# An image block with a selective scan and attention: rotation by partition halves, unrolled attention, and SyncE's scan-stage jobs in thirds

## The chip, the cores and the metric

The kernel runs on one core of one Trainium2 chip. The metric is the device time of a run in microseconds (us), lower is better. A core has TensorE (PE in the profile; its weight loads are PEld), VectorE (DVE), ScalarE (ACT), GpSimd (POOL) and SyncE (SP), which here only issues DMAs.

## The reference

The input is four images of 32x32 tokens with 384 channels, in float32. Two residual blocks follow one another: `x = x + scan_block(groupnorm(x))`, then `x = x + attention(groupnorm(x))`. The first is a projection, a 3x3 convolution, a selective scan over 1024 tokens in four directions, a norm, a gate and a projection back. The second is attention with 12 heads of width 32 over 1024 tokens, a rotation of q and k, and a position bias from two tables:

```python
qkv = x.reshape(B, L, dim) @ w_qkv + b_qkv           # q, k, v: 12 heads of 32
def rot(t):                                          # neighbours (2i, 2i+1) of a head are a pair
    t0, t1 = tr[..., 0], tr[..., 1]
    return stack([t0 * c - t1 * s, t0 * s + t1 * c], axis=-1)
attn = einsum('bnqd,bnkd->bnqk', rot(q), rot(k)) * scale
rel_h = einsum('bnhwc,hkc->bnhwk', q6, bias_h)       # one value per key row
rel_w = einsum('bnhwc,wkc->bnhwk', q6, bias_w)       # one value per key column
attn = attn + rel_h[..., :, None] + rel_w[..., None, :]
out = softmax(attn) @ v                              # then w_proj, b_proj
```

## The kernel before

Channels lie on the 128 partitions and the 1024 tokens along the free axis. The work has two stages.

**Scan stage.** 384 items (4 images, 6 channel tiles, 16 states) run in one unrolled order. For an item SP loads a broadcast row of B into one of three buffers (`load_b`, L476), POOL multiplies it (`times_b`, L1617) into one of three further buffers, ACT makes the decay (L1459), DVE scans (L1091) and multiplies by C (L1099), and TensorE broadcasts C (L577) and adds up (L586). Tables of due items (`PE_FRONT`, `DVE_MID`, `SP_MID` and so on) say after which item of an image each engine does the work for the next image ("front") and the previous one ("mid"). SP's tables hold whole-image jobs: `next_x` loads the next input (1.5 MB), `x_load` the residual, `x1_store` and `xn2_store` store the residual before and after the second group norm. Every engine works its queue in order, so each job of SP stands ahead of the B loads behind it, and so does each wait of a job.

**Attention stage.** A hardware loop over the four images (`Fori`). At its end every engine increments `image_done` and waits until SP has cleared the semaphores and opened the next image (`leave_image`). Within an image TensorE first does `START`: products for q and k of head group 0 (L570), the rotation's neighbour swap (`turn`, a product with a +-1 matrix, L844), the value products (L820), and the position-bias products (`rel`, L861) on both tables, of which the column-table result is also transposed (`relw`, L851). Then 96 steps follow, 32 for each of three groups of four heads. A step is: scores of two steps ahead (L888), perhaps one job of `JOBS` for a later group, half of the product with v on odd steps (L913), and eight transposes of the probabilities (L899). DVE adds one bias and takes the row maximum (L1216), ACT exponentiates (L1543), both save transposes (L1170, L1520). The other bias comes in through 32 more rows of the score product: SP copies q, k and the bias rows of each head into 128-partition operands `QX` and `KX` (L537, L545), beside a one-hot pattern. A job's result goes through PSUM bank 7, so a job waits until the previous one has been saved.

The rotation before: ACT saves q or k half (`RAW`, L1512), TensorE swaps neighbours (L844), DVE multiplies the swapped PSUM tile by sine (L1134), POOL multiplies `RAW` by cosine (L1647) and adds both (L1654). A head's 32 channels are 32 neighbouring partitions.

Of the kernel before, what the change touches and what calls it, by code (L numbers as in the profile page):

```python
# [8 lines left out]
P = 128  # L9
# [74 lines left out]
SP_FRONT = {("next_x",): 50, ("z_store",): 75, ("b_store",): 80, ("bcs",): 90}  # L84
SP_FIRST = {**SP_FRONT, ("z_store",): 78}
SP_MID = {("x_load",): 1, ("z_load",): 2, ("x1_store",): 62, ("xn2_store",): 82}
# [30 lines left out]
ATT_MATS = {"w_qkv": (3 * P, 3 * C), "cos": (P, L), "sin": (P, L), "turn": (P, P), "head_rows": (NH, C),  # L117
# [7 lines left out]
class Signal:  # L125


    def __init__(self, sem, unit=1):
        self.sem, self.unit = sem, unit

    def after(self, b, n):

        return n * self.unit
# [6 lines left out]
def build(nc, x, mats, cols, sel_in, onehot, b_rows, z_rows, x1, xn2, out):  # L140
    ctx = ExitStack()
    with ctx:
# [3 lines left out]
        def signal(name, per_image=0, unit=1):  # L146
            return Signal(ctx.enter_context(nc.semaphore(name)), unit)
# [96 lines left out]
        RELC = from_mats(30, 4).rearrange("p (g a) l -> p g a l", g=2)  # L244
        RELW = [from_mats(25)[:, 0, :], RELC[:, 0, 1, :], RELC[:, 1, 1, :]]
# [15 lines left out]
        image_done = ctx.enter_context(nc.semaphore("image_done"))  # L261
        clearing = ctx.enter_context(nc.semaphore("clearing"))
        image_open = ctx.enter_context(nc.semaphore("image_open"))
# [6 lines left out]
        xn_loaded = signal("xn_loaded", unit=16)  # L270
# [36 lines left out]
        x_loaded = signal("x_loaded", unit=16)  # L307
# [5 lines left out]
        turn_psum = signal("turn_psum", 4 * GROUPS)  # L313
        sin_done = signal("sin_done", 4 * GROUPS)
        rope_ready = signal("rope_ready", 4 * GROUPS)
        rel_psum = signal("rel_psum", 12)
        rel_saved = signal("rel_saved", 12)
        relw_psum = signal("relw_psum", 2 * GROUPS)
        relw_saved = signal("relw_saved", 2 * GROUPS)
# [28 lines left out]
        per_image = range(x_loaded.sem.num, dve_step.sem.num + 1)  # L348

        def leave_image(eng, b):  # L350

            eng.sem_inc(image_done, 1)
            eng.wait_ge(image_open, b + 1)

# [8 lines left out]
        def turned_place(s):  # L363
# [5 lines left out]
        JOBS = [[(kind, n) for kind in ("proj", "turn", "rel") for n in range(4)]  # L369
                + [("relw", 0), ("relw", 1)],  # L370
                [("proj", 4), ("proj", 5), ("turn", 4), ("turn", 5), ("proj", 6), ("proj", 7), ("turn", 6),
                 ("turn", 7), ("proj", 8), ("proj", 9)] + [("rel", n) for n in range(4, 12)]
                + [("turn", 8), ("turn", 9)] + [("relw", n) for n in range(2, 6)],
                [("proj", 10), ("proj", 11), ("turn", 10), ("turn", 11)]]


        START = [(m, ()) for m in range(5)] + [(5, (0,)), (6, ()), (7, (1,)), (8, (2,)), (9, (3,)), (10, (4,)),
                                               (11, (5,)), (None, (6, 7)), (12, ()), (13, ())]

        JOB_AT = [{2 + m * 6 // 5: m for m in range(len(JOBS[1]))}, {6 + 4 * m: m for m in range(len(JOBS[2]))}, {}]  # L380

        ROPE_FOR, REL_FOR = [4, 10, 12], [4, 12, 12]
# [29 lines left out]
        def _(sp):  # L412
# [10 lines left out]
            def front(f, what):  # L423
                if what == "next_x":
                    sp.wait_ge(z_psum.sem, z_psum.at(2 * f + 2))
# [21 lines left out]
            def mid(m, what):  # L447
                if what == "x_load":
                    if m:
                        sp.wait_ge(xn2_stored.sem, xn2_stored.at(m))  # L450
# [1339 lines left out]
```

## Time and profile before

| what | value |
|---|---|
| median of three runs | 3247.94 us (3243.51 to 3249.18) |
| profiled execution: its own time | 3243.84 us |
| its span | 3242.3 us |
| busy share: PE, DVE, ACT, POOL | 86%, 68%, 50%, 41% |
| mean granted TensorE clock | 0.959 of full |
| DMA over the span | 298.70 MB |

The shares are means over two stages that differ. The scan stage runs to about 1740 us; there DVE is the busiest engine. In the attention stage, from about 1740 us on, it is TensorE.

### The profile page before, as it was taken

To read this page: it belongs to the slowest core of one execution; us is meant where nothing else is said; L and a number is where in the kernel's file an instruction comes from. 1 tells how busy PE (TensorE), PEld (TensorE's weight loads), DVE (VectorE), ACT (ScalarE), POOL (GpSimd) and SP (SyncE) were. 2 spreads that over 40 slices of the span, in tenths; PEclk is the share of its full clock that TensorE was granted. 3 is DMA by queue.
4 is the path that set the end of the run, shared out by engine and by line. 5 is a ranking of instruction groups with operands and counts; after the bars stand their busy time and mean duration, and the time that the engine had idled before them with its cause. 6 is when DMAs were issued, how large, how long until landed. Compare 5 with 4: busy or idle time off the path is not lost. (4 is left out here: it accounts for less than half of the span.)

```text
span 3242.3 us, 40875 instructions
## 1 busy us (share of the span) xinstructions
PE 2795.6 (86%) x16024; PEld 1414.8 (44%) x16024; DVE 2199.8 (68%) x2149; ACT 1619.9 (50%) x1972; POOL 1339.3 (41%) x624
## 2 busy tenths in 40 slices
PE   6479678878798777787768999999998999989999
PEld 2133233323343332232224565556554665556655
DVE  0398898988989889899862566525664366625665
ACT  2555655555546555464521456424663356515564
POOL 0587877877778777786731100011000100011000
PEclk9799999998999989999887999999999999999999
DMA  2334544454444545444533011020111111020110
GB/s 74 117 141 117 162 147 159 139 140 151 150 161 137 148 144 181 152 139 137 197 107 91 1 34 53 11 63 1 34 53 42 32 34 38 16 72 1 34 53 21
DMA packets 93559, 298.70 MB, mean 92 GB/s; under 512 B 15693, under 2 KB 18521, under 8 KB 93241
## 3 DMA queue, kind: packets, MB, share of 16 engines
q1 hardware_dynamic: 93368, 296.07, 29.4%
q8 instruction: 132, 2.16, 0.3%
q14 instruction: 59, 0.48, 0.0%
HBM read 239.91 MB, written 23.07 MB: 81 GB/s over the span
## 5 line engine op out<-in xcount | busy, mean ns | idle before, releaser
L1617 POOL TENSOR_TENSOR arena<-arena 128x1024 f32<-128x1024 f32 x384 | 901.6, 2357 | 348.3 <-DVE arena L1091 230.9
L1091 DVE TENSOR_TENSOR_SCAN arena<-PS,arena 128x1024 f32<-128x1024 f32 x384 | 879.0, 2289 | 145.0 <-ACT PS L1459 71.6
L586 PE MATMUL PS<-arena,ident 128*128 128x512 f32 x1536 | 772.3, 627 | 14.7 <-ACT arena L1470 12.5
L1459 ACT ACTIVATE PS<-arena,a_inf,a_neg 128x1024 f32<-128x1024 f32 x384 | 463.8, 1208 | 620.3 <-DVE arena L1091 614.3
L1216 DVE CUSTOM_DVE_ANT_1 arena<-PS,arena 128x1024 f32<-128x1024 f32 x384 | 467.4, 1219 | 345.0 <-PE PS L888 345.0
L1543 ACT ACTIVATE arena<-arena,neg_max 128x1024 f32<-128x1024 f32 x384 | 441.1, 1149 | 509.2 <-DVE neg_max L1216 509.2
L577 PE MATMUL PS<-arena,sel 96*128 96x512 bf16 x768 | 241.6, 397 | 325.5 <-DVE arena L1099 321.9
L1099 DVE TENSOR_TENSOR arena<-arena,PS 128x1024 f32<-128x1024 f32 x384 | 460.7, 1200 | 54.0 <-PE PS L577 52.7
L888 PE MATMUL PS<-arena 64*128 64x512 f32 x1536 | 432.5, 641 | 8.8 <-DMA arena<-arena 8.7
L586 PEld LDWEIGHTS PS<-arena,ident 128*128 128x128 f32 x1536 | 306.1, 200 | 279.4 <-issue 225.6
L899 PE MATMUL PS<-ident,arena 128*128 128x128 f32 x3072 | 413.3, 278 | 2.6 <-ACT arena L1543 2.6
L1647 POOL TENSOR_TENSOR arena<-arena 128x512 f32<-128x512 f32 x48 | 61.0, 1271 | 831.9 <-ACT arena L1512 831.9
L899 PEld LDWEIGHTS PS<-ident,arena 128*128 128x128 f32 x3072 | 336.6, 142 | 145.3 <-issue 87.5
L577 PEld LDWEIGHTS PS<-arena,sel 96*128 96x128 bf16 x768 | 55.4, 99 | 613.2 <-DVE arena L1099 540.0
L1170 DVE COPY arena<-PS 128x1024 f32<-128x1024 f32 x192 | 233.8, 1218 | 70.0 <-PE PS L899 64.8
L1654 POOL TENSOR_TENSOR arena<-arena 128x512 f32<-128x512 f32 x48 | 61.0, 1271 | 432.6 <-DVE arena L1134 431.7
L1520 ACT ACTIVATE arena<-PS 128x1024 f32<-128x1024 f32 x192 | 193.2, 1006 | 45.7 <-PE PS L899 45.7
L913 PEld LDWEIGHTS PS<-arena 128*32 128x32 f32 x6144 | 156.3, 110 | 127.2 <-issue 117.3
L913 PE MATMUL PS<-arena 128*32 128x128 f32 x6144 | 206.7, 276 | 0.0
L570 PE MATMUL PS<-normed,arena 128*128 128x512 f32 x288 | 141.8, 638 | 21.8 <-issue 21.0
L888 PEld LDWEIGHTS PS<-arena 64*128 64x128 f32 x1536 | 116.4, 185 | 76.8 <-issue 65.5
L861 PEld LDWEIGHTS PS<-arena 128*128 128x128 f32 x1024 | 124.9, 192 | 38.0 <-issue 24.2
(126 smaller groups left out, 2314.7 us busy)
## 6 DMA issues: line engine op xcount, KB each, us to landing
arena<-b_rows SPq DMA_DIRECT2D x256, 512.0 KB, 3.8
arena<-b_rows SPq DMA_DIRECT2D x256, 256.0 KB, 3.9
arena<-arena SPq DMA_DIRECT2D x192, 128.0 KB, 2.9
arena<-arena SPq DMA_DIRECT2D x120, 64.0 KB, 2.0
normed<-xn SPq DMA_DIRECT2D x5, 1536.0 KB, 6.7
normed<-x_in SPq DMA_DIRECT2D x4, 1536.0 KB, 7.1
residual<-x_in SPq DMA_DIRECT2D x4, 1536.0 KB, 9.3
x<-residual SPq DMA_DIRECT2D x4, 1536.0 KB, 6.5
```

Source lines behind the costliest of these rows:

```text
L577: last = pe.matmul(dst[:, half(h)], lhs, rhs(h), start=(k == 0), stop=(k == len(pairs) - 1))
L586: last = pe.matmul(dst[:, half(h)], lhs, rhs[:, half(h)], start=start, stop=stop, skip_group_check=True)
L888: last = pe.matmul(scores_place(s)[:, h * HALF:(h + 1) * HALF], QX[rows, j, qb * P:(qb + 1) * P], KX[rows, j, :], start=True, stop=True)
L899: last = pe.transpose(turned_place(s)[:, t * P:(t + 1) * P], PR[s % 3][:, t * P:(t + 1) * P], idn)
L913: last = pe.matmul(banks(6, 1)[HD * j:HD * j + HD, (n % 2) * P:(n % 2 + 1) * P], V[:, t, head * HD:(head + 1) * HD], PT[:, n % 2, j, t, :] ...
L1091: dve.tensor_tensor_scan(HS[:, at % 2, ::step], DA[:, ::step], DBU[:, at % R3, ::step], 0.0, ALU.mult, ALU.add).then_inc(scan_done.sem, 1)
L1099: dve.tensor_tensor(HC[:, at % R_HC, :], HS[:, at % 2, :], C_PSUM, ALU.mult).then_inc(hc_ready.sem, 1)
L1170: dve.tensor_copy(PT[:, n % 2, s % HG, :, :], turned_place(s).rearrange("p (t q) -> p t q", t=QB)).then_inc(pt_saved[0].sem, 1)
L1216: dve.tensor_tensor_reduce(out=PR[s % 3].rearrange("p (h w) -> p h w", w=IMG), in0=scores_place(s).rearrange("p (h w) -> p h w", w=IMG), i ...
L1459: act.activation(DA, DELTA[:, tile % 2, :], ACT.Exp, bias=a_inf[:, col:col + 1], scale=a_neg[:, col:col + 1]).then_inc(da_ready.sem, 1)
L1543: act.activation(PR[s % 3], PR[s % 3], ACT.Exp, bias=neg_max[:, s % 4:s % 4 + 1], scale=-1.0, accum_out=row_sum[:, qb, at:at + 1]).then_in ...
L1617: pool.tensor_tensor(DBU[:, at % R3, :], DU[:, tile % 2, :], BSB[:, at % R3, :], ALU.mult).then_inc(dbu_ready.sem, 1)
```

## The change

Four things change together.

1. **Rotation by halves.** The columns of `w_qkv` (and `b_qkv`, and the bias tables' rows) are permuted so that a head lies in every fourth partition and a pair's partner lies 64 partitions away. The swap is then no product: DVE multiplies the lower half of `RAW` by sine into the upper half of `RT2` and the other way round, two 64x512 operations from SBUF in place of one 128x512 from PSUM. The `turn` matrix and its 12 products per image are gone. SP's copies read `QKC[j::HG]` and not a block of 32 partitions.
2. **The tables trade places.** The column table now goes through the score product, and the row table is added by DVE (the broadcast of `bias` runs along the other axis). The row-table bias is made with q as the weights (`relh`: 16 products of 32 columns by 128, dealt over four blocks of 32 output partitions), directly in transposed form. So half of the `rel` products and all `relw` transposes are gone, and six `relh` jobs per image come in.
3. **No loop and no barrier.** The four images are written out one after the other; semaphores count on over the images (`Signal.after` adds `b * per_image`), and `leave_image` is gone.
4. **SP's scan-stage jobs.** Each 1.5 MB load or store is three of 0.5 MB, mostly due two items apart and all jobs due later than before.

```diff
-SP_FRONT = {("next_x",): 50, ("z_store",): 75, ("b_store",): 80, ("bcs",): 90}
-SP_MID = {("x_load",): 1, ("z_load",): 2, ("x1_store",): 62, ("xn2_store",): 82}
+SP_FRONT = {("next_x", 0): 54, ("next_x", 1): 56, ("next_x", 2): 58, ("z_store",): 79, ("b_store",): 84, ("bcs",): 92}
+SP_MID = {("x_load", 0): 20, ("x_load", 1): 22, ("x_load", 2): 24, ("z_load",): 10, ("x1_store", 0): 65,
+          ("x1_store", 1): 67, ("x1_store", 2): 69, ("xn2_store", 0): 83, ("xn2_store", 1): 86, ("xn2_store", 2): 88}
...
                     if f + 1 < B:
-                        load_image(XN[:, :, :], x, f + 1, xn_loaded.sem)
-                    else:
-                        sp.wait_ge(xn2_stored.sem, xn2_stored.at(1))
+                        load_tile(XN, x, f + 1, k, xn_loaded[k].sem)
+                    elif k == 0:
+                        sp.wait_ge(xn2_stored.sem, xn2_stored.at(CT))
                         load_image(XN[:, :, :], xn2, 0, normed_loaded)
...
-                    elif kind == "turn":
-                        pe.wait_ge(raw_saved.sem, raw_saved.after(b, n + 1))
-                        pe.matmul(dst, W["turn"][:, 0, :], RAW[n if n < 4 else n % 2], start=True, stop=True
-                                  ).then_inc(turn_psum.sem, 1)
-                    elif kind == "relw":
+                    elif kind == "relh":
                         g, h = divmod(n, 2)
-                        pe.wait_ge(rel_saved.sem, rel_saved.after(b, 12 if g else 4))
-                        for t in range(QB // 2):
-                            at = h * HALF + t * P
-                            last = pe.transpose(dst[:, t * P:(t + 1) * P], RELC[:, g // 2, 1, at:at + P], idn)
+                        pe.wait_ge(rope_ready.sem, rope_ready.after(b, (2, 6, 8)[g]))
+                        for r in range(IMG // 2):
+                            at = h * IMG // 2 + r
+                            t, row = divmod(r, HG)
+                            last = pe.matmul(dst[IMG * row:IMG * row + IMG, t * P:(t + 1) * P],
+                                             QKC[:, PLACE[g, "q"], at * IMG:(at + 1) * IMG],
+                                             W["rel_h"][:, 0, HG * (IMG - 1 - at):HG * (REL - at)],
+                                             start=True, stop=True, skip_group_check=True)
...
-                        dve.tensor_tensor(RT2[:, h, :], src, W["sin"][:, 0, half(h)], ALU.mult
+                        dve.tensor_tensor(RT2[0:XT, h, :], raw[XT:P, :], W["sin"][XT:P, 0, half(h)], ALU.mult)
+                        dve.tensor_tensor(RT2[XT:P, h, :], raw[0:XT, :], W["sin"][0:XT, 0, half(h)], ALU.mult
                                           ).then_inc(sin_done.sem, 1)
...
-            with pe.Fori(0, B) as b:
+            for b in range(B):
...
-                leave_image(pe, b)
```

What moves on TensorE at the start of an image. Before, from the products for q and k up to the second table product (L570 is q and k, L844 the swap, L820 values, L861 the tables):

```order
L570 MATMUL PS<-normed,arena 128x512 x12
L844 MATMUL PS<-arena 128x512 x2
L820 MATMUL PS<-arena,normed 128x384 x3
L844 MATMUL PS<-arena 128x512 x2
L820 MATMUL PS<-arena,normed 128x384 x3
L861 MATMUL PS<-arena 128x32 x2
L820 MATMUL PS<-arena,normed 128x384
L861 MATMUL PS<-arena 128x32 x4
```

The changed kernel at the same place, up to the first score product (L561 is q and k, L814 values, L854 the column table, L843 the row table with q as weights, L880 the scores):

```order
L561 MATMUL PS<-normed,arena 128x512 x12
L814 MATMUL PS<-arena,normed 128x384 x6
L854 MATMUL PS<-arena 128x32 x2
L814 MATMUL PS<-arena,normed 128x384
...
L854 MATMUL PS<-arena 128x32 x4
L843 MATMUL PS<-arena 32x128 x32
L814 MATMUL PS<-arena,normed 128x384 x6
L880 MATMUL PS<-arena 128x512 x6
```

The swaps are gone, two table jobs of four are left with two value blocks in each, and the last two value blocks now stand directly ahead of the scores.

On DVE, the first operations of an image before (L1134 sine, L1156 table copies, L1161 copies of the transposed table):

```order
L1134 TENSOR_TENSOR arena<-PS,arena 128x512 x4
L1139 ISA
L1156 COPY arena<-PS 128x512 x2
L1156 COPY arena<-PS 128x32x16 x2
L1161 COPY arena<-PS 128x512 x2
```

And in the changed kernel (L1125 and L1126 are the two halves of sine):

```order
L1125 TENSOR_TENSOR arena<-arena 64x512
L1126 TENSOR_TENSOR arena<-arena 64x512
...
L1125 TENSOR_TENSOR arena<-arena 64x512
L1126 TENSOR_TENSOR arena<-arena 64x512
L1141 COPY arena<-PS 128x32x16 x2
L1146 COPY arena<-PS 128x512 x2
```

Four sine operations from PSUM have become eight from SBUF, and two table copies have gone.

## Rows read from the trace of the kernel before

**Rows 1.** The page: busy time and share of the span by engine.
```profile
PE 2795.6 (86%) x16024; PEld 1414.8 (44%) x16024; DVE 2199.8 (68%) x2149; ACT 1619.9 (50%) x1972; POOL 1339.3 (41%) x624
```

**Rows 2.** Windows: stretch, busy PE, PEld, DVE, ACT, POOL, clock, DMA share, GB/s.
```profile
131.00:1650.00 1519.00, 1205.33 (x3050) 485.86 (x3051) 1341.27 (x873) 830.83 (x762) 1174.67 (x506) 0.95 0.48 151
2116.50:2493.00 376.50, 364.68 (x3176) 219.49 (x3176) 204.61 (x303) 179.93 (x284) 30.19 (x24) 0.99 0.13 35
```

**Rows 3.** Waits of PE, 1760 to 3242 us: total, times, longest.
```profile
PE PS L570 <- issue: 21.0, 3, 7.0
```

**Rows 4.** The chain that ended last: start, us, what.
```profile
1739.89 13.38 PE PS L570 x24
...
2116.55 12.79 PE PS L570 x24
2129.34 1.72 PE PS L844 x4
```

**Rows 5.** Timeline at the start of image 2: start, us, what.
```profile
2137.57 0.97 PE L861 MATMUL PS<-arena 128*128 128x32 f32 x8
...
2138.38 0.89 PE L820 MATMUL PS<-arena,normed 128*128 128x384 f32 x2
...
2139.11 0.97 PE L861 MATMUL PS<-arena 128*128 128x32 f32 x8
...
2163.35 1.13 PE L888 MATMUL PS<-arena 64*128 64x512 f32 x4
```

**Rows 6.** Timeline of PE in the steps of image 2.
```profile
2221.11 2.00 PE L861 MATMUL PS<-arena 128*128 128x64 f32 x16
2222.94 1.04 PE L899 MATMUL PS<-ident,arena 128*128 128x128 f32 x8
...
2226.90 1.08 PE L913 MATMUL PS<-arena 128*32 128x128 f32 x32
2227.91 1.09 PE L899 MATMUL PS<-ident,arena 128*128 128x128 f32 x8
...
2262.90 1.13 PE L844 MATMUL PS<-arena 128*128 128x512 f32 x2
2263.86 1.04 PE L899 MATMUL PS<-ident,arena 128*128 128x128 f32 x8
...
2268.98 0.66 PE L851 MATMUL PS<-ident,arena 128*128 128x128 f32 x4
2269.47 1.04 PE L899 MATMUL PS<-ident,arena 128*128 128x128 f32 x8
```

**Rows 7.** Waits of DVE and POOL, 140 to 1650 us: total, times, longest.
```profile
DVE arena L1091 <- POOL arena L1617: 43.4, 18, 6.9
...
POOL arena L1617 <- DMA arena<-b_rows: 113.4, 16, 13.8
```

**Rows 8.** Timelines of SP, POOL and DVE around two whole-image loads.
```profile
319.58 0.39 SPq L421 DMA_DIRECT2D normed<-x_in  x1
...
329.63 4.64 POOL L1617 TENSOR_TENSOR arena<-arena 128x1024 f32<-128x1024 f32 x2 [11.74 <-DMA arena<-b_rows]
...
332.06 2.29 DVE L1091 TENSOR_TENSOR_SCAN arena<-PS,arena 128x1024 f32<-128x1024 f32 x1 [6.93 <-POOL arena L1617]
...
1109.42 2.29 DVE L1091 TENSOR_TENSOR_SCAN arena<-PS,arena 128x1024 f32<-128x1024 f32 x1 [6.03 <-POOL arena L1617]
```

**Rows 9.** Groups by line and shape: busy us, mean ns, idle before.
```profile
L1647 POOL TENSOR_TENSOR arena<-arena 128x512 f32<-128x512 f32 x48 | 61.0, 1271 | 831.9 <-ACT arena L1512 831.9
...
L913 PE MATMUL PS<-arena 128*32 128x128 f32 x6144 | 206.7, 276 | 0.0
...
L1134 DVE TENSOR_TENSOR arena<-PS,arena 128x512 f32<-128x512 f32 x48 | 33.0, 688 | 84.0 <-PE PS L844 82.3 <-POOL arena L1654 1.7
...
L1187 DVE TENSOR_SCALAR arena<-arena,b_qkv 128x512 f32<-128x512 f32 x24 | 11.7, 487 | 0.9
```

**Rows 10.** DMA queues, 2110 to 2490 us: packets, MB, share of 16 engines.
```profile
q8 instruction: 27, 0.44, 0.5%
```

More of the change, by code:

```diff
@@ L267, in build @@
         onehot_loaded = signal("onehot_loaded", unit=16)
-        xn_loaded = signal("xn_loaded", unit=16)
+        xn_loaded = [signal(f"xn_loaded_{k}", unit=16) for k in range(CT)]
         gn1_stats, gn1_psum, gn1_var, gn1_rstd = [signal(f"gn1_{k}") for k in ("stats", "psum", "var", "rstd")]
@@ L478, in load_b @@
                                  ).then_inc(b_loaded[i % R3].sem, 16)
-            load_image(XN[:, :, :], x, 0, xn_loaded.sem)
+            for k in range(CT):
+                load_tile(XN, x, 0, k, xn_loaded[k].sem)
             for name in COLS:
@@ L502, in _ @@
                         load_mats(ATT_MATS, att_loaded)
-            mid(B - 1, "x_load")
+            for k in range(CT):
+                mid(B - 1, "x_load", k)
             sp.wait_ge(dbu_ready.sem, dbu_ready.at(ITEMS * B))
@@ L811, in _ @@
             pe.wait_ge(onehot_loaded.sem, onehot_loaded.at(2 * HG))
-            with pe.Fori(0, B) as b:
+            for b in range(B):
                 pe.wait_ge(normed_loaded, 16 * (b + 1))
@@ L819, in value_product @@
                         pe.wait_ge(v_saved.sem, v_saved.after(b, t - 3))
+                    elif t == 0 and k == 0 and b:
+                        pe.wait_ge(pj_read.sem, pj_read.after(b, 0))
                     last = pe.matmul(banks(t % 4, 1)[:, 0:C], XN[:, k, t * P:(t + 1) * P],
@@ L1121, in _ @@
             dve.wait_ge(att_loaded.sem, att_loaded.at(len(ATT_MATS)))
-            with dve.Fori(0, B) as b:
-                link = steps(dve, dve_step)
+            link = steps(dve, dve_step)
+            for b in range(B):
                 def job(phase, m):
@@ L1229, in _ @@
                     biased_scores(s)
-                    if k - 2 in JOB_AT[g]:
-                        job(g + 1, JOB_AT[g][k - 2])
+                    for after, kinds in ((4, ("proj",)), (2, ("rel", "relh"))):
+                        if k - after in JOB_AT[g] and JOBS[g + 1][JOB_AT[g][k - after]][0] in kinds:
+                            job(g + 1, JOB_AT[g][k - after])
                     if g + 1 == GROUPS and k - 2 in LATE_AT:
@@ L1494, in _ @@
                 mid(B - 1, *job)
-            with act.Fori(0, B) as b:
+            for b in range(B):
                 def save_v(t):
@@ L1640, in _ @@
             pool.wait_ge(att_loaded.sem, att_loaded.at(len(ATT_MATS)))
-            with pool.Fori(0, B) as b:
+            for b in range(B):
                 for n in range(2 * len(PREPARED)):
@@ L1714 @@
     mats["w_out"] = wo
-    mats["w_qkv"] = np.asarray(L1_conv_w_qkv)
+    pos = np.arange(P)
+    paired = HD * (pos % HG) + 2 * (pos % XT // HG) + pos // XT
+    qkv_order = np.arange(3 * C)
+    for k in range(2 * GROUPS):
+        qkv_order[k * P:(k + 1) * P] = k * P + paired
+    mats["w_qkv"] = np.asarray(L1_conv_w_qkv)[:, qkv_order]
     mats["w_proj"] = np.asarray(L1_conv_w_proj)
@@ L1721 @@
     ang = np.concatenate([(tok % IMG).astype(f)[:, None] * freqs, (tok // IMG).astype(f)[:, None] * freqs], 1)
[L1722 to L1724 removed]
+    mats["cos"] = np.cos(ang).T[pos % XT // HG]
+    mats["sin"] = np.sin(ang).T[pos % XT // HG] * np.where(pos < XT, 1, -1)[:, None]
     mats["ident"] = np.eye(P)
@@ L1735 @@
     mats["last_taps"] = diag[:, 16:18].reshape(P, 2 * P)
-    turn = np.zeros((P, P), f)
-    for i in range(0, P, 2):
-        turn[i + 1, i] = -1.0
-        turn[i, i + 1] = 1.0
-    mats["turn"] = turn
     mats["chan_mean"] = np.full((P, P), 1.0 / DI)
```

209 lines of the change are left out of this document (89 added, 120 removed).

## The prediction, written before the run

> **What bounds the kernel now.** I read the busy shares first [rows 1]: TensorE leads with 86%, DVE has 68%. Such a mean is no bound, so I cut the span by stage [rows 2]. From 131 to 1650 us DVE is busy 1341.3 of 1519 us and TensorE 1205.3: the scan stage goes at DVE's pace, and what counts there is what DVE waits for. An image of attention takes 376.5 us, of which TensorE is busy 364.7, DVE 204.6, ACT 179.9 and POOL 30.2. There each product that goes from TensorE's queue is time won, and DVE has some 170 us per image in which to hide work. The waits of DVE in the scan stage [rows 7] say how much of it SP can be blamed for: DVE stood 43.4 us for POOL's product (18 times), and POOL stood 113.4 us for B rows. The timeline around one case [rows 8] shows the chain: SP issues a whole-image load at 319.58, POOL then gets no B row for 11.74 us, and DVE, which POOL had run ahead of by its buffers, stands for the last 6.93 us. Last comes the border between images: three times TensorE waits 7.0 us for nothing that the profile shows, before its first product [rows 3]; that is the barrier. After it the 24 product passes take 12.79 us [rows 4].
>
> **The swap products.** 12 per image leave. At the start four of them take 3.4 us (two in 1.72 [rows 4]). In the steps one takes 0.96 us from its start to that of the transposes behind it [rows 6]: eight give 7.7 us.
>
> **The table products.** At the start, four jobs each go with one value block. Eight passes take 0.81 us up to the start of the next value pair, and a value pair 0.73 us [rows 5]; so a job of 32 passes is 3.3 us and a value block of three pairs 2.2 us, 5.5 us together, four times 22 us. After the change two jobs carry two blocks each: 2 x (3.3 + 4.4) = 15.4 us. Saved: 6.6 us. In the steps a job of 16 passes takes 1.83 us (2221.11 to 2222.94 [rows 6]); four of eight leave: 7.3 us.
>
> **Transposes against the new row-table products.** A transposing job takes 0.49 us [rows 6]. A new job is 16 products in two passes, 32 passes with 32-column weights and 128 columns moving, dealt over four blocks of output partitions. The trace has that very form in the product with v: 32 passes in 1.01 us (2226.90 to 2227.91 [rows 6]). I take 1.0 us. Six jobs so cost 6 x 0.5 = 3 us more, 1.0 of it at the start and 2.0 in the steps. The bounds: 32 passes at the group's mean duration of one, 0.276 us [rows 9], if none overlapped, would be 8.8 us a job; below, no less than the 0.49 of the transposes.
>
> **A new wait at the start.** The last two value blocks now stand right ahead of the scores, which wait for the last value copy of ACT. Before, the transposes stood between. An estimate of 0.7 us from the copy and its signals.
>
> **The barrier.** The wait of 7.0 us goes, three times [rows 3]; about 0.1 of it is normal turnaround, so 6.9. With it goes the slow clock behind it: 24 passes take 12.79 us [rows 4], where four passes of the same length take 1.72 us [rows 4], so 24 should take 10.3. I take 2.4 us, three times. The first image starts out of the scan stage's tail at the same slow pace (13.38 us [rows 4]), which stays. The loop's code was already fetched anew per image: 27 blocks, 0.44 MB, in an image's window [rows 10]. Written-out code needs the same blocks, so I cost it at nothing.
>
> **Sine on DVE.** 24 operations of 64x512 from SBUF per image, in place of 12 of 128x512 from PSUM at 0.688 us [rows 9]. No row shows the new form. It costs no less than the one-input 0.487 and no more than POOL's 1.271 for 512 elements [rows 9]; since the length is the same as in the old one, I take 0.65, 7 us more per image. The table copies that leave (two of 512 at the start, eight of 256 in the steps) give about 5 back at the old sine's pace. The net lies in DVE's idle 170 us; if that cover were gone, it would cost 2 us per image. In the chain of an image's start the two first rotated halves are ready about 8.8 us in (products 12 x 0.43, copy an estimated 0.9, cosine and sum 2 x 1.27), and TensorE wants them after 24 passes and two value blocks, 10.3 + 4 = 14.3. The head copies on SP follow the table's save at about 30 us; by estimate a first head then needs some 4 us, and the scores stand at 36.
>
> One rule speaks against this. In the trace POOL's two operations around sine take 1.271 us each while DVE's sine reads PSUM [rows 9]. The Trainium skill, "SBUF — State Buffer", section "SBUF: two separate sides", has it that a DVE operation with two SBUF inputs and a GpSimd operation that reads SBUF hold a shared port pair in turn, and the other fully blocks. No run here shows that yet, since every large DVE operation of before has one input in PSUM. By that rule sine and cosine of a half, which start on the same signal, would run one after the other.
>
> **SP's thirds.** Of DVE's 43.4 us for POOL [rows 7] one case stays as it is: the load at the third image's turn, which brings the normed image, is still whole (6.03 us at 1109.42 [rows 8]). The other 37.4 come with whole-image jobs or with SP waiting at a job that is due too early. A third takes SP as many issues but a third of the queue time: of 11.74 us of POOL's stall about 4 remain, and the 6.93 that reached DVE show that POOL's lead of 4.8 us covers those. SP's jobs are due 4 items later, where their inputs are ready. I take 32 of 37.4. Two more issues of 0.39 us [rows 8] stand at the very start: +0.9.
>
> **The sum.** Start of an image: 3.4 + 6.6 - 1.0 - 0.7 = 8.3, and 2.4 for the clock in images 2 to 4. Steps: 7.7 + 7.3 - 2.0 = 13.0. Four times 21.3 is 85.2; three times 6.9 + 2.4 is 27.9; attention gives 113.1. With 32 and -0.9 from the scan stage it is 144.2. The profiled execution took 3243.84 us, 4.1 below the median of the runs; so 3099.6 beside it, 3103.7 beside the median. I predict **3103 us**. Its own range is 3085 to 3122: the scan stage's part between 20 and 42 (a little behind the stalls too), the steps' part some 2 us per image either way.
>
> **The rivals.**
>
> *Scan stage without gain.* The stalls move: 0.5 MB still delays a B row, POOL's lead is used up by three of them in six items, or DVE stands for ACT instead. For it: [rows 7] name POOL, not the queue, for the wait, and 70 of the 113.4 us were hidden already. Against it: the long stalls begin with whole-image jobs. Time: 3103 + 32 = 3135. Chance 0.11.
>
> *The lock costs TensorE.* By it a half needs 2 x 1.27 + 2 x 0.65 = 3.8 us, so the second rotated half is ready at about 11.2 us, still ahead of 14.3, and nothing is lost there. In the steps the pair on DVE takes up to 3.9 us instead of 1.3, and the next bias and exponential come later. TensorE's lead is two steps of 2.6 us (scores 1.1, transposes 1.0, half of 1.0 for v [rows 5, 6]), more where a q or k product lies between; against it stand bias and exponential, which are less than DVE's and ACT's mean load of a step, 204.6 / 96 = 2.1 and 1.9 us [rows 2]. Were the 2.6 us of each of the eight jobs to show in full, it would be 21 us per image and 3187; half of that, 3145, is the more likely size. This mechanism is what the skill's page named above would bring if its rule is hard. Chance 0.07.
>
> *Another wait takes over in the steps.* A job waits for the save of the job before, and scores for head copies. If half of the steps' gain (6.5 per image) goes so: 3129. Chance 0.06.
>
> *More than forecast.* Stalls of the scan stage also lower the clock behind them; with that gone 15 us more: 3088. It lies in the range. Chance 0.10.
>
> *Slower: the 32-column products don't overlap.* The mean duration of one is 0.276 us [rows 9] against 0.032 between starts [rows 6]. There are 768 passes over four images; at 0.276 apiece they cost 187 us more, and the time is 3290. It decides from 0.19 us more a pass on. Against it: the form is that of the product with v, in the same order of blocks. Chance 0.02.
>
> **How the numbers follow.** The forecast keeps 0.64; with the case of more it is 0.74 below 3125. The range **3082 to 3140** takes in the scan rival and half of the others. A measurement of this kernel can tell about 0.2% (6.5 us) from no change. Only the last rival is slower, and nothing ends near 3248: faster 0.97, same 0.01, slower 0.02.
>
> **What would show it.** An image's period near 345 us in place of 376.5; no wait of 7 us ahead of L561 (q and k) at the border, and its 24 passes in 10.3 us; 16 new products (L843) in 1.0 us; DVE's wait for POOL in the scan stage at 6 to 15 us in place of 43.4, with 6 us of it near the third image's whole load. The sine operations show at 0.6 to 0.7 us, or by the rule at up to 1.9 with POOL's beside them longer. Wrong would be: waits of TensorE for ACT's exponential in steps with sine jobs, for head copies at the first scores, or POOL still waiting 8 to 13 us for B rows.

## The result, and the profile after

The changed kernel takes **3092.28 us** (median of 4 runs, 3089.48 to 3094.16); the kernel before took 3245.73 us on the same chip (4 runs, 3242.41 to 3249.18). The ratio is 0.953, with a 95% interval of 0.951 to 0.954. The forecast was 3103 us in a range of 3082 to 3140. The profiled execution took 3094.16 us, with a span of 3092.4.

The windows of the changed kernel by stage: the same stretch of the scan stage as in [rows 2], then image 2 of attention (stretch, busy PE, PEld, DVE, ACT, POOL, clock, DMA share, GB/s).

```profile
131.00:1650.00 1519.00, 1223.54 (x3116) 494.98 (x3116) 1361.94 (x885) 840.81 (x771) 1183.50 (x509) 0.96 0.48 153
...
2048.10:2394.50 346.40, 339.08 (x3194) 202.69 (x3193) 215.30 (x305) 178.68 (x284) 32.76 (x24) 1.00 0.15 38
```

Image 2 took 376.5 us in [rows 2] and takes 346.4 (the others 349.5, 347.4 and 350.4). TensorE's busy time fell by 25.6 of those 30.1 us (364.68 to 339.08); the rest are waits that are gone, the 7 us at the border first. DVE rose by 10.7 us and stays at 62% of an image. In the scan stage more work is done in the same 1519 us (DVE 1361.9 busy in place of 1341.3), and attention begins at 1698.56 where it began at 1739.89 [rows 4].

The chain that ended last, at the border between images 1 and 2 (start, us, what):

```profile
2045.30 2.84 PE PS L948 x6
2048.14 10.30 PE PS L561 x24
2058.44 3.87 PE PS L814 x12
...
2077.13 1.88 PE PS L843 x64
2079.01 4.08 PE PS L814 x12
2083.11 0.50 ACT arena L1483
...
2083.66 1.15 PE PS L880 x4
```

The last projection of image 1 (L948) ends at 2048.14, and the q and k products of image 2 (L561) start there. They take 10.30 us, where those of [rows 4] took 12.79. From their start to the first scores (L880) it is 35.5 us, against 46.8 in [rows 4, 5]. The two row-table jobs (L843) take 1.88 us together, and the value save of ACT (L1483) holds the scores for 0.57 us: the new wait of the prediction, at 0.7.

The 41.3 us by which attention begins earlier and the 108.6 us by which it is shorter (1502.4 to 1393.8) make up the 149.9 us between the two spans. Part by part, with the forecast of the prediction's own steps:

| part | forecast | traces |
|---|---|---|
| scan stage, with the issues at the start | 31.1 | 41.3 |
| start of an image, clock included, four | 40.4 | 41.8 |
| barrier and border, three | 20.7 | 20.9 |
| steps and end of an image, four | 52.0 | 45.9 |
| sum | 144.2 | 149.9 |

The starts are 8.9 us in image 1 (from 47.5 to 38.6) and 11.3, 10.7 and 10.9 in the others (from 46.8, 46.3 and 46.4 to 35.5 each); the borders are the 6.88, 7.03 and 7.01 us between L956's end and L570's start; the steps are what is left of 108.6.

What DVE and POOL of the changed kernel wait for in the scan stage, 140 to 1620 us (total, times, longest):

```profile
DVE arena L1081 <- ACT PS L1442: 70.4, 285, 1.5
DVE arena L1089 <- PE PS L568: 56.4, 65, 3.3
...
DVE arena L1081 <- POOL arena L1599: 0.5, 3, 0.2
...
POOL arena L1599 <- DMA arena<-b_rows: 6.4, 3, 4.1
```

DVE's wait for POOL (43.4 us in [rows 7], 40.6 of it before 1620) is 0.5 us, and POOL's for B rows fell from 113.4 to 6.4. The prediction had left 6 to 15 us of the first.

What TensorE waits for in the attention stage, 1690 us to the end:

```profile
PE PS L880 <- DMA arena<-arena: 12.8, 12, 1.7
PE PS L948 <- DVE arena L1172: 6.8, 4, 1.7
PE PS L880 <- ACT arena L1503: 4.1, 4, 1.0
PE PS L891 <- ACT arena L1526: 3.6, 4, 0.9
...
PE PS L880 <- ACT arena L1483: 2.3, 4, 0.6
```

The 21.0 us of [rows 3] are gone. The scores' wait for head copies was 8.7 us (8 times) in the same view of the kernel before and is 12.8 now; the wait for L1503, ACT's save of the transposed probabilities, is new. The experiments take both apart.

### The profile page after: what moved, and what is told of

Same layout as the page of the kernel before. It is cut to its first block and busy times, and to the rows that moved or that the text cites. A ratio compares the mean times of both kernels' runs of the same rounds, so it can differ in the third digit from the quotient of the medians.

```text
span 3092.4 us, 40835 instructions
## 1 busy us (share of the span) xinstructions
PE 2684.6 (87%) x16088; PEld 1346.6 (44%) x16088; DVE 2242.5 (73%) x2157; ACT 1614.7 (52%) x1972; POOL 1351.2 (44%) x624
## 5 line engine op out<-in xcount | busy, mean ns | idle before, releaser
L577 PE MATMUL PS<-arena,ident 128*128 128x512 f32 x1536 | 762.0, 620 | 15.0 <-ACT arena L1453 12.8
L1629 POOL TENSOR_TENSOR arena<-arena 128x512 f32<-128x512 f32 x48 | 68.4, 1425 | 955.2 <-ACT arena L1495 955.2
L880 PE MATMUL PS<-arena 64*128 64x512 f32 x1536 | 431.6, 640 | 19.3 <-DMA arena<-arena 12.8
L577 PEld LDWEIGHTS PS<-arena,ident 128*128 128x128 f32 x1536 | 302.5, 198 | 275.0 <-issue 221.4
L1503 ACT ACTIVATE arena<-PS 128x1024 f32<-128x1024 f32 x192 | 192.7, 1004 | 19.4 <-PE PS L891 19.4
L880 PEld LDWEIGHTS PS<-arena 64*128 64x128 f32 x1536 | 116.5, 185 | 88.5 <-issue 59.0
L1636 POOL TENSOR_TENSOR arena<-arena 128x512 f32<-128x512 f32 x48 | 64.0, 1333 | 176.3 <-DVE arena L1126 175.7
L561 PE MATMUL PS<-normed,arena 128*128 128x512 f32 x288 | 135.7, 615 | 0.6 <-DVE g_tmp L1025 0.6
L577 PE MATMUL PS<-arena 128*128 128x512 f32 (+1 forms) x224 | 108.3, 622 | 12.0 <-ACT arena L1305 5.5
```

Source lines behind the costliest of these rows:

```text
L561: last = pe.matmul(dst, lhs, rhs(h), start=(k == 0), stop=(k == len(pairs) - 1))
L577: last = pe.matmul(dst[:, half(h)], lhs, rhs[:, half(h)], start=start, stop=stop, skip_group_check=True)
L880: last = pe.matmul(scores_place(s)[:, h * HALF:(h + 1) * HALF], QX[rows, j, qb * P:(qb + 1) * P], KX[rows, j, :], start=True, stop=True)
```

## The experiments

All diffs are against the changed kernel. Beside each run stands the ratio to the kernel before on the same chip, with its 95% interval.

### The scan stage: the size of SP's jobs or their time

Four edits of SP's table. In two of them a 1.5 MB transfer is one job again; in two all jobs are due when they were due before, in one the next input's load alone.

**whole_late**: whole-image jobs at the new times.

```diff
-SP_FRONT = {("next_x", 0): 54, ("next_x", 1): 56, ("next_x", 2): 58, ("z_store",): 79, ("b_store",): 84, ("bcs",): 92}
+SP_FRONT = {("next_x", 0): 54, ("z_store",): 79, ("b_store",): 84, ("bcs",): 92}
...
+SP_MID = {("x_load", 0): 20, ("z_load",): 10, ("x1_store", 0): 65, ("xn2_store", 0): 83}
```

> The changed kernel with SP's whole 1.5 MB loads and stores back, at the new, later due items (next_x 54, x_load 20, x1_store 65, xn2_store 83). Theory 'size' (a whole transfer ahead of the B rows starves POOL, the thirds cure it): DVE waits again 25 to 43 us for POOL in the scan stage, time about 3092 + 30 = 3122. Rival 'lateness' (SP stood at jobs whose inputs were not ready, and only the later due items cure it): DVE's wait for POOL stays under 6 us and the time is within 5 us of 3092. The changed kernel's one load that was left whole did not stall DVE, which speaks for the rival; I lean to it, 3095.

Measured: 3093.99 us (3089.6 to 3097.44), ratio 0.953 (0.951 to 0.955). The same as with thirds. POOL waits more for its rows, but nothing of it reaches DVE (waits, 140 to 1620 us):

```profile
DVE arena L1082 <- POOL arena L1600: 0.5, 3, 0.2
...
POOL arena L1600 <- DMA arena<-b_rows: 31.3, 8, 6.2
```

So the size, on which my term rested, is worth nothing that can be measured once the jobs are late enough. POOL stands up to 4.5 us behind a 1.5 MB load at which SP hadn't waited, and up to 6.2 us behind a store at which it had; its lead over DVE, 6.9 us in most places of the kernel before (13.79 us of POOL's wait against 6.84 of DVE's at 713.73), covers that.

**thirds_early**: thirds, at the old times.

```diff
+SP_FRONT = {("next_x", 0): 50, ("next_x", 1): 52, ("next_x", 2): 54, ("z_store",): 75, ("b_store",): 80, ("bcs",): 90}
...
+SP_MID = {("x_load", 0): 1, ("x_load", 1): 3, ("x_load", 2): 5, ("z_load",): 2, ("x1_store", 0): 62,
+          ("x1_store", 1): 64, ("x1_store", 2): 66, ("xn2_store", 0): 82, ("xn2_store", 1): 84, ("xn2_store", 2): 86}
```

> The changed kernel with thirds, two items apart, but starting at the old due items (next_x 50, 52, 54; x_load 1, 3, 5; x1_store 62, 64, 66; xn2_store 82, 84, 86; z_store 75, b_store 80, bcs 90). Theory 'size': DVE's wait for POOL stays under 8 us, time within 6 us of 3092. Rival 'lateness': SP waits at next_x, b_store, bcs and xn2_store with B loads behind it, DVE waits 20 to 35 us for POOL, time 3112 to 3127.

Measured: 3111.7 us (3108.74 to 3117.66), ratio 0.959 (0.957 to 0.962). DVE waits 15.7 us for POOL (8 times, longest 6.6), less than the 20 to 35 expected of lateness alone and more than the under 8 of size alone.

**whole_early**: whole-image jobs at the old times, SP's tables of before in the changed kernel.

> The changed kernel with the whole of SP's scan-stage part undone (whole transfers at the old due items). Both theories: DVE's wait for POOL in the scan stage is back at 43 us, the attention stage begins about 41 us later than in the changed kernel, and the time is 3092 + 41 = 3133 (3128 to 3138). If the parts did not add up, it would lie outside that.

Measured: 3137.69 us (3134.61 to 3144.59), ratio 0.968 (0.965 to 0.970). DVE waits 39.0 us for POOL, and attention begins at 1739.48, as in [rows 4]. With this run the change splits in two: SP's tables are worth 45 us by the medians (41 by the traces), the rest of the change 106 (110 by the traces).

The waits of SP itself say what is early. In the kernel before, 140 to 1620 us:

```profile
SPq L460 <- DVE residual L1071: 48.9, 3, 16.3
SPq L421 <- PE PS L586: 43.6, 3, 14.6
SPq L464 <- ACT residual L1275: 25.2, 3, 10.4
SPq L444 <- ACT arena L1379: 24.6, 3, 10.5
SPq L438 <- ACT arena L1369: 23.2, 3, 9.3
SPq L433 <- POOL arena L1578: 10.6, 1, 10.6
```

And in the changed kernel:

```profile
SPq L468 <- POOL arena L1599: 6.4, 2, 3.9
SPq L440 <- ACT arena L1364: 6.3, 3, 2.4
SPq L416 <- ACT residual L1260: 4.5, 3, 1.7
```

SP stood 176 us at jobs whose input wasn't there yet, up to 16.3 us at a time, with the B loads behind it in its queue; now it is 17.8, with 0.3 us each left of the loads' waits for L577. Thirds without the delay gave 26 of the 45 us, in two ways. A third can go when its third of the input is ready, so thirds alone shorten some of these waits: in thirds_early the wait of 48.9 us, for the residual before its store, is 26.6, and that of 25.2 is 11.3. And size does count where SP is late already. At the load of the next input SP waits 14.6 us in whole_early as in thirds_early; what DVE then stands differs (timeline of DVE, whole_early first):

```profile
330.31 2.29 DVE L1082 TENSOR_TENSOR_SCAN arena<-PS,arena 128x1024 f32<-128x1024 f32 x1 [6.12 <-POOL arena L1600]
```

```profile
328.39 2.29 DVE L1081 TENSOR_TENSOR_SCAN arena<-PS,arena 128x1024 f32<-128x1024 f32 x1 [3.14 <-POOL arena L1599]
```

At the second such load it is 6.52 us against 3.64; at the third, which is whole in both kernels, 6.34 against 6.60. So of the 23.3 us by which DVE's waits fell between the two runs some 6 come from size at an equal wait of SP. The other 17 come at the stores, where SP's waits and the transfers are both shorter; the runs don't part the two there.

**next_early**: of all jobs only the load of the next input at its old time.

```diff
-SP_FRONT = {("next_x", 0): 54, ("next_x", 1): 56, ("next_x", 2): 58, ("z_store",): 79, ("b_store",): 84, ("bcs",): 92}
+SP_FRONT = {("next_x", 0): 50, ("next_x", 1): 52, ("next_x", 2): 54, ("z_store",): 79, ("b_store",): 84, ("bcs",): 92}
```

> The changed kernel with one job of SP's scan stage moved back: the next input's thirds at items 50, 52, 54 in place of 54, 56, 58. In thirds_early three of DVE's four long waits for POOL (3.1, 3.6 and 6.6 us) followed that job. Theory 'SP stands at a job that is not ready': the wait for the z products, with B loads queued behind it, makes them, so DVE waits 12 to 15 us for POOL and the time is 3092 + 15 = 3107, nearly all of what thirds_early lost. Rival: several jobs share the loss, and this one alone gives under 6 us, 3094 to 3098.

Measured: 3109.7 us (3106.6 to 3111.28), ratio 0.958 (0.956 to 0.960): 17 us of the 19 that thirds_early lost, as the theory had it. Its waits, 140 to 1620 us:

```profile
DVE arena L1081 <- POOL arena L1599: 13.7, 5, 6.6
...
SPq L413 <- PE PS L577: 29.1, 2, 14.6
SPq L410 <- PE PS L577: 14.5, 1, 14.5
```

The load may only begin when TensorE has read the last of the old input for the z products (L577). Four items too early, and SP stands 14.5 us at each of three such loads with every B load behind it. POOL then waits 8.5, 10.0 and 13.6 us for a B row, and DVE, which it had run 4.8 us ahead of once and 6.9 twice, stands for the 3.6, 3.1 and 6.6 us left; the 6.6 are behind the load that is whole.

### The border: the barrier or the loop

**barrier_no_loop**: images written out, but all engines meet after each as before.

```diff
+        def leave_image(eng, b):
+            eng.sem_inc(image_done, 1)
+            eng.wait_ge(image_open, b + 1)
...
+                sp.wait_ge(image_done, 4 * b + 4)
+                sp.sem_inc(image_open, 1)
...
                     project(m, (2,)).then_inc(pj_psum.sem, 1)
+                leave_image(pe, b)
```

> The changed kernel, still written out without a loop, but with a barrier at each image's end: each engine signals and waits until SP, after all four, opens the next image. Theory 'barrier': the meeting of the engines cost the 7 us, so TensorE waits about 7 us at each border, with the slow clock behind it, time 3092 + 3 x 9 = 3119. Rival 'loop': 5.2 us of the 7 came after SP had opened the next image, so they belong to the loop's jump and the code behind it; then TensorE waits only 1.5 to 2 us per border, and the time is 3096 to 3100. I lean to the rival.

Measured: 3098.52 us (3098.44 to 3105.47), ratio 0.956 (0.953 to 0.958). The chain at the first border:

```profile
2046.34 2.86 PE PS L956 x6
...
2049.22 0.76 DVE arena L1188
...
2050.43 0.02 SPq L559
...
2050.49 10.57 PE PS L569 x24
```

From the end of the projection to the next product it is 1.29 us: DVE's last addition, the store's issue, the release. The products behind it take 10.57 us at a granted clock of 1.00, so the clock isn't slow there. In the kernel before the same chain had a release at 2111.32 and then 5.23 us in which TensorE waited for nothing that the profile shows:

```profile
2111.23 0.09 SPq L558
2111.32 5.23 issue
```

From the end of the projection (2109.67) to that release it was 1.65 us, with the clearing of the semaphores, which barrier_no_loop leaves out. The passes behind it ran at half the full clock first (windows from the start of L570, all 24 passes and the first 3.45 us of them):

```profile
2116.55:2129.34 12.79, 12.79 (x25) 5.67 (x26) 0.00 (x0) 2.06 (x3) 1.26 (x1) 0.82 0.30 116
2116.55:2120.00 3.45, 3.45 (x4) 1.50 (x5) 0.00 (x0) 0.00 (x0) 0.00 (x0) 0.50 0.96 376
```

In the changed kernel the granted clock of the 24 passes is 1.00. So of the 9.4 us at this border (6.9 of waiting and 2.5 in the passes) the meeting of the engines is 1.3 to 1.65; the other 7.7 come with the hardware loop: the 5.23 us after the release and the slow passes behind them. What within the loop's turn takes the 5.23 us no run shows.

### The head copies ahead of the scores

SP issues 24 copies for the next head group in 16 us at each of the eight group changes within images (changed kernel, timeline of SP):

```profile
2177.77 16.00 SPq L542 DMA_DIRECT2D arena<-arena  x24
```

**block_rows**: q and k are copied from 32 neighbouring partitions in place of every fourth. The heads so get other channels than theirs; the transfers' count and size are the same.

```diff
-                    q, k = QKC[j::HG, PLACE[g, "q"], :], QKC[j::HG, PLACE[g, "k"], :]
+                    rows = slice(HD * j, HD * j + HD)
+                    q, k = QKC[rows, PLACE[g, "q"], :], QKC[rows, PLACE[g, "k"], :]
```

> The changed kernel with SP's copies of q and k read from 32 neighbouring partitions, as before, and not from every fourth; the bytes are the same, but the heads' channels are wrong ones, so only the time means something. Theory 'stride': the copies land later because of the every-fourth-partition source (median 3.1 to 3.3 us against 2.7 before), so with blocks the landing falls to 2.7, TensorE's waits for head copies fall from 12.8 to 8 or 9 us, and the time is 3086 to 3090. Rival: the landing is longer for another reason and these waits are set by SP's 24 issues of 0.6 us one after another; then nothing moves, 3090 to 3094.

Measured: 3093.11 us (3092.45 to 3094.17), ratio 0.953 (0.951 to 0.954). The copies do land sooner: by the median 2.9 us at 128 KB and 2.0 at 64 KB, where the changed kernel has 3.3 and 2.6. But TensorE waits for them as long as ever (13.6 us, 13 times). Part of that may be the issues, which took a little longer here (17.00 us for the same 24), so this run speaks against the landing as the bound without settling it.

**keys_on_act**: a third of these copies, those of k, are issued by ACT.

```diff
-                        for dst, src in operands(g, j):
+                        for dst, src in operands(g, j)[0:2] + operands(g, j)[4:6]:
                             sp.dma_start(dst, src).then_inc(head_loaded[j].sem, 16)
...
+                    if k >= STEPS - HG and g + 1 < GROUPS:
+                        if j == 0:
+                            act.wait_ge(rope_ready.sem, rope_ready.after(b, ROPE_FOR[g + 1]))
+                        key = QKC[j::HG, PLACE[g + 1, "k"], :]
+                        for dst, src in ((KX[0:HD, j, :], key[:, 0:HALF]), (KX[2 * HD:3 * HD, j, :], key[:, HALF:L])):
+                            act.dma_start(dst, src).then_inc(head_loaded[j].sem, 16)
```

> The changed kernel with the two k copies of each head for groups 1 and 2 issued by ACT right behind its exponential of that head's last step, instead of by SP. Theory 'issue': TensorE's waits for head copies (12.8 us before products, 17.5 before weight loads) come from SP's 24 issues in 16 us at each of eight group changes; with 16 issues they fall under 4 us and the time is 3092 - 12 = 3080. Rival 'ACT pays': each issue holds ACT about 0.6 us as it does SP, the exponentials come late, TensorE waits for ACT instead, and the time is 3090 to 3100.

Measured: 3086.17 us (3083.83 to 3087.33, 5 runs), ratio 0.950 (0.949 to 0.952). TensorE's wait for the copies, 1690 us to the end:

```profile
PE PS L880 <- DMA arena<-arena: 5.0, 5, 1.4
```

The wait for the copies fell from 12.8 to 5.0 us, though each takes longer to land (4.2 us at 128 KB, 4.8 on ACT's queue). So the landing isn't what sets that wait; what fell is the time in which SP issues a group's copies, 11.98 us for 16 in place of 16.00 for 24. The expectation was a wait under 4 us and 3080; 5.0 us are left, and the span fell by 7.7 us (3092.4 to 3084.7), as much as this wait.

**half_on_act**: the third copy of q too, 12 on each queue.

> As keys_on_act, with one of the two q copies of each head on ACT's queue too: three copies of six on each queue. Theory 'issue': TensorE's remaining waits for head copies (5.0 and 7.2 us) go to near nothing, 3086 - 5 = 3081. Rival 'transfers share the engines': the landing, which grew to 4.2 and 4.8 us when two queues issued, is the bound now, and nothing is won, 3084 to 3088. Rival 'ACT pays': 3088 to 3100.

Measured: 3098.47 us (3096.83 to 3101.59, 5 runs), ratio 0.955 (0.953 to 0.956). Worse than no such edit. ACT's timeline at a group change:

```profile
2186.74 1.02 ACT L1503 ACTIVATE arena<-PS 128x1024 f32<-128x1024 f32 x1 [1.65 <-issue]
```

Three issues of 0.5 to 1.4 us per step are more than ACT has free: it is idle 1.65 us ahead of its save, 1.44 of them in an issue, and the scores' wait for L1503 rises to 10.3 us (18 times). Nor did the wait for copies fall: it is 8.7 us (5 times, longest 3.7) where keys_on_act has 5.0. SP's 12 issues are stretched over 11.27 us, 4.0 of them waits for scores, and the copies on ACT's queue land after 4.9 and 5.3 us. So fewer issues on SP help only as far as the copies don't come late from elsewhere.

### Sine and cosine on one port

**cos_after_sin**: POOL waits for the sine of a half before its cosine.

```diff
                     pool.wait_ge(raw_saved.sem, raw_saved.after(b, n + 1))
+                    pool.wait_ge(sin_done.sem, sin_done.after(b, n + 1))
```

> The changed kernel with POOL's cosine product waiting for DVE's sine of the same half, so that the two never run at once. Theory 'shared port': the sine operations that took up to 1.75 us fall back to 0.69 and the cosine ones from 1.43 to 1.27 in the mean, at no cost of time since nothing on TensorE waits for them: 3092, within 3. Rival 'slow source': the longer sine operations come from the partition shift or the buffers themselves; then they stay long. Rival 'chain': the rotation at an image's start stands on the path, and the serial order shows as 1 to 4 us per image: 3096 to 3108.

Measured: 3092.55 us (3091.58 to 3094.78), ratio 0.953 (0.951 to 0.954). The means fell only in part (L1125 853 to 776 ns, L1126 1011 to 928), since POOL's sum of one half still meets the sine of the next.

**never_together**: DVE waits for the sum of the half before as well.

```diff
-                        if n >= 2:
-                            dve.wait_ge(rope_ready.sem, rope_ready.after(b, n - 1))
+                        if n >= 1:
+                            dve.wait_ge(rope_ready.sem, rope_ready.after(b, n))
...
+                    pool.wait_ge(sin_done.sem, sin_done.after(b, n + 1))
```

> As cos_after_sin, and DVE's sine also waits until POOL's sum of the half before is done, so that DVE's sine and POOL's products never overlap at all. In cos_after_sin the means fell only part of the way (sine 853 and 1011 ns to 776 and 928, cosine 1425 to 1313). Theory 'shared port': now every sine operation takes 0.69 us and every POOL one 1.27. Rival 'slow source': some stay long. Time within 4 us of 3092, since this is hidden at an image's start and in the steps.

Measured: 3093.16 us (3091.63 to 3093.99), ratio 0.953 (0.951 to 0.954). Groups by line (busy us, mean ns, idle before), first the changed kernel, then this one:

```profile
L1629 POOL TENSOR_TENSOR arena<-arena 128x512 f32<-128x512 f32 x48 | 68.4, 1425 | 955.2 <-ACT arena L1495 955.2
...
L1125 DVE TENSOR_TENSOR arena<-arena 64x512 f32<-64x512 f32 x48 | 40.9, 853 | 16.2 <-ACT arena L1495 14.9
```

```profile
L1630 POOL TENSOR_TENSOR arena<-arena 128x512 f32<-128x512 f32 x48 | 61.0, 1271 | 1139.5 <-DVE arena L1126 1139.5
...
L1125 DVE TENSOR_TENSOR arena<-arena 64x512 f32<-64x512 f32 x48 | 33.0, 687 | 49.3 <-POOL arena L1637 34.3 <-ACT arena L1495 14.0
```

The other half of sine went from 1011 to 685 ns, the sum on POOL from 1333 to 1271. Kept apart, all four are at their own pace: the two engines did hold each other up, and it cost no time.

### The new wait for ACT's save

The wait for L1503 comes once in an image, at 2239.81 us in image 2. DVE's timeline ahead of it in the changed kernel:

```profile
2233.79 0.69 DVE L1125 TENSOR_TENSOR arena<-arena 64x512 f32<-64x512 f32 x1
2234.49 0.69 DVE L1126 TENSOR_TENSOR arena<-arena 64x512 f32<-64x512 f32 x1
2235.20 1.23 DVE L1155 COPY arena<-PS 128x1024 f32<-128x1024 f32 x1
2236.34 1.22 DVE L1201 CUSTOM_DVE_ANT_1 arena<-PS,arena 128x1024 f32<-128x1024 f32 x1
```

Both sines and the copy of transposed probabilities stand ahead of the bias. **sine_later** moves the sines of the steps one step on, where no copy comes between them and the next bias:

```diff
-                    for after, kinds in ((4, ("proj",)), (2, ("rel", "relh"))):
+                    for after, kinds in ((5, ("proj",)), (2, ("rel", "relh"))):
```

> The changed kernel, with DVE's two sine operations of a half one step later: behind the bias of an odd step, where the next thing in DVE's queue is a bias, instead of behind that of an even step, where the copy of the transposed probabilities (1.23 us) still comes ahead of the next bias. Theory: TensorE's new wait of 4.1 us (4 times 1.0) for ACT's save L1503 goes back to the second sine operation: at 2233.79 DVE does sine (0.69), sine (0.69) and the copy (1.23) in a row, so the bias starts at 2236.34, the exponential at 2237.60 and ACT's save, which the scores at 2239.81 wait for, ends late. Then the wait falls from 4.1 to under 1 us and the time to about 3088.5 (between 3086 and 3091). Rival: the wait comes from ACT's own load at this place or from TensorE's shorter queue; then 4.1 us stay and the time is 3092, or more if the rotated halves come too late.

Measured: 3089.58 us (3089.23 to 3090.42, 5 runs), ratio 0.953 (0.951 to 0.954). The wait for L1503 is gone from the list of waits, and attention takes 1391.1 us in place of 1393.8 (span 3087.4, start 1696.26). The trace settles where the wait came from; the ratio can't tell 2.7 us from none.

**keys_and_sine**: this edit and that of keys_on_act.

> The last edit together with the key copies on ACT's queue, which alone gave 3086.2. If the two gains are of separate waits they add up: about 3082.5 (TensorE's waits for DMA at the scores at 5 us as there, those for L1503 under 1 us). If ACT is what is short with the copies on its queue, L1503 stays at 4 to 5 us and the time is 3086.

Measured: **3081.90 us** (3079.34 to 3084.86, 5 runs), ratio 0.950 (0.949 to 0.952). TensorE waits 6.2 us for head copies and 0.6 for L1503. It is the lowest median of all, 10 us below the changed kernel's; but the kernel before, timed beside it, was 3.5 us quicker than beside keys_on_act, so the ratios of the two (0.9503 and 0.9504) don't tell the sine's part. The traces do: attention takes 1382.7 us (span 3079.2, start 1696.54) where keys_on_act has 1386.7 (3084.7, 1698.04), so the two gains add up, 7.1 and 4.0.

## Why the prediction was right, and where its sizes were off

The forecast of 3103 us was 11 us too high, inside the likeliest case's own range. Beside the profiled execution it was 5.4 too high (3099.6 against 3094.16); the rest lies in how the two profiled executions stand to their medians.

**Swap products, tables, row-table jobs: as said.** The start takes 35.5 us; 46.8 less the 8.3 and 2.4 of the prediction is 36.1. In the steps a column-table job takes 1.87 us, and the new form overlaps like the product with v (timeline of TensorE):

```profile
2170.54 1.08 PE L843 MATMUL PS<-arena 128*32 128x128 f32 x32
2171.55 1.09 PE L891 MATMUL PS<-ident,arena 128*128 128x128 f32 x8
```

From start to start it is 1.01 us. The rival in which these products don't overlap falls here.

**The barrier and the clock: right in size, wrong in name.** The wait went and the 24 passes take 10.30 us. But "that is the barrier" was wrong: the meeting is 1.3 to 1.65 of the 6.9 us. The prediction read a wait "for nothing that the profile shows" as the barrier, while the chain had the answer: the engines were released at 2111.32, and 5.23 us of issue came after.

**Instruction supply at nothing: no trace speaks against it.** The images written out start without a gap, and the instruction queue of [rows 10] moved 128 packets over the whole span in place of 132.

**Sine: the row was right in the steps, the rule at the start.** (That every large DVE operation of before has an input in PSUM holds for those with two inputs; L1187 of [rows 9] has its one in SBUF.) While POOL is idle a sine of 64x512 takes 0.69 us, close to the 0.65 taken. At an image's start sine and cosine go together (timeline of DVE, then of POOL):

```profile
2051.48 0.69 DVE L1125 TENSOR_TENSOR arena<-arena 64x512 f32<-64x512 f32 x1 [2.54 <-ACT arena L1495]
2052.18 1.66 DVE L1126 TENSOR_TENSOR arena<-arena 64x512 f32<-64x512 f32 x1
```

```profile
2051.52 1.77 POOL L1629 TENSOR_TENSOR arena<-arena 128x512 f32<-128x512 f32 x1 [161.29 <-ACT arena L1495]
```

The first sine takes its 0.69 us, to 2052.17. Cosine, issued with it, ends at 2053.29, which is 1.1 us after the sine's end and so about its own 1.27. The second sine shows 1.66 us and ends at 2053.84, 0.55 us after cosine. They go one after the other. The Trainium skill, "SBUF — State Buffer", section "SBUF: two separate sides", has one of the two block the other fully; the trace agrees, within 0.2 us. The second rotated half was ready at about 2059.3 (POOL's second sum ends there), 11.2 us into the image, which is the later of the two times in the prediction, and still ahead of the 14.3 at which TensorE wants it. In the steps POOL is idle beside most sines. So the rival by which the lock costs TensorE is out: never_together takes the lock away and gains nothing.

**Steps: 45.9 us in place of 52.0.** Here the rival of another wait came true in small. The head copies' wait rose by 4.1 us; keys_on_act shows that it hangs on the 16 us of 24 issues on SP and not on the landing. Those issues took as long before (16.62 us in image 2), so it rose for another reason: that a shorter group leaves less time to hide them is likely and not shown. The other 4.1 us are the wait for L1503: the second sine delays one bias per image, as sine_later shows. The prediction put the sine's net cost at nothing because DVE has 170 us of idle time in an image; that cover was there on the mean and not at this one step.

**Scan stage: 41.3 us in place of 31.1.** The step that was off is the one that took the queue time of a transfer as the cause: "a third takes SP as many issues but a third of the queue time". whole_late shows that size gives nothing once the jobs are late, next_early that a job due before its input is ready is what stops the B loads. Beside such a job the queue time did count: a third made DVE's stand 3 us shorter at each of two loads, where the prediction let a third's stall vanish behind POOL's lead. The prediction named the jobs' lateness in one sentence and gave it no price. By the same error it kept 6.03 us for the whole load of the third image; that load is still whole and no longer stalls DVE, because it too is due later. With all 43.4 us of DVE's wait taken away and 0.9 for the issues, the term would have been 42.5. That the sum came within 5.7 us of the traces is in part luck: the scan stage gave 10 us more than its term and the steps 6 less.

The rival by which the scan stage gains nothing is out; the case of more came in part, though by stalls that went and not, so far as the rows show, by the clock (0.96 against 0.95 in that stretch).

## What to carry to other kernels

Before you price a transfer's size, read the waits of the queue that issues it: a job that stands for an input holds back everything behind it, and a later place in the table may be worth all that splitting seems to promise. Here splitting helped only while the jobs were too early. A wait for nothing that the profile shows is named by the chain just ahead of it, here by the time between the release and the next product. Idle time of an engine hides new work only where it lies; look at what stands ahead of the next critical operation at that step.

## What the runs showed of the hardware

- A hardware loop's turn cost TensorE 5.23 to 5.39 us after the release, and the 24 passes behind it 12.24 to 12.79 us (granted clock 0.86 to 0.82) in place of 10.30 (1.00); a meeting of all engines in written-out code cost 1.3 us, with passes of 10.57 us at 1.00.
- The issue of a copy to 32 partitions took SP 0.67 us on average (16.00 us for 24), and this bounded head copies of 64 and 128 KB that land in 2.6 and 3.3 us. On ACT an issue took 0.47 to 1.44 us of an engine that computes.
- Source partitions in steps of four made the 128 KB copies land in 3.3 us in place of 2.9, and those of 64 KB in 2.6 in place of 2.0 (medians, block_rows against the changed kernel).
- In the scan stage a 1.5 MB transfer made one job cost as little as three of 0.5 MB when SP didn't stand before it (3093.99 us against 3092.28), and 26 us more when it did (3137.69 against 3111.7).
- DVE and POOL, both multiplying from SBUF, went one after the other where they met: operations of 0.69 and 1.27 us show as 1.66 and 1.77; kept apart, they were back at 0.69 and 1.27.
